# Splitting the negated row maxima on GpSimd instead of VectorE in a two-layer gated cross-attention kernel

## The reference, cut to what matters

```python
scores = jnp.einsum('bhqd,bhkd->bhqk', q, k) / jnp.sqrt(jnp.float32(HD))
scores = jnp.where(mask, jnp.float32(-1000000000000000.0), scores)   # layer 0 alone
attn = jax.nn.softmax(scores, axis=-1)
ctx = jnp.einsum('bhqk,bhkd->bhqd', attn, v)
```

## Time and profile before

| what | value |
|---|---|
| median of 3 runs | 342.97 us (339.25 to 344.19) |
| the profiled execution | 341.92 us |
| its span, first to last instruction | 339.7 us |
| PE busy | 280.9 us (83%) |
| VectorE busy | 213.8 us (63%) |
| ScalarE busy | 170.8 us (50%) |
| GpSimd busy | 92.1 us (27%) |

### The profile page before, as it was taken

How to read it: one execution, slowest core, us unless ns; L and a number is a source line. 1 busy time by engine, 2 the same in 40 slices (tenths; PEclk the granted TensorE clock), 3 DMA queues, 4 the chain that set the end, 5 groups by cost and what they waited for, 6 DMA issues and landing times.

```text
span 339.7 us, 7944 instructions
## 1 busy us (share of the span) xinstructions
PE 280.9 (83%) x2982; PEld 208.4 (61%) x2982; DVE 213.8 (63%) x658; ACT 170.8 (50%) x331; POOL 92.1 (27%) x158
## 2 busy tenths in 40 slices
PE   1723879899999999986999987899978887889870
PEld 0311556687778778764486465776766776768650
DVE  2310785676685676574447564774976885987890
ACT  1311226566655665645654542254767674676530
POOL 3510141152142241311000110431423431641450
PEclk9965878999999999999899999855999998999995
DMA  8366447444443332000000034344434443000121
GB/s 227 96 185 166 111 131 209 134 128 125 117 117 121 88 114 69 6 2 0 2 0 0 3 91 140 88 123 139 115 113 130 137 122 98 4 5 3 33 61 32
DMA packets 27679, 30.48 MB, mean 90 GB/s; under 512 B 13715, under 2 KB 24820, under 8 KB 26484
## 3 DMA queue, kind: packets, MB, share of 16 engines
q1 hardware_dynamic: 20446, 27.12, 27.6%
q10 hardware_dynamic: 4188, 2.47, 2.9%
q0 software_dynamic: 3008, 0.39, 0.8%
HBM read 22.43 MB, written 7.14 MB: 87 GB/s over the span
## 4 chain that ended last, share of the span: by engine, by line
PE 59%; DMA 12%; DVE 10%; POOL 6%; issue 5%; ACT 4%; ACTq 1%; SPq 1%; DVEq 0%; POOLq 0%
PE bank L1219 8%; DMA QS<-nmT 7%; PE bank L1189 6%; PE bank L1167 6%; PE bank L1311 5%; PE bank L1185 4%; PE bank L1163 4%; DMA QS<-qparts 3%; PE bank L1263 3%; PE bank L1227 3%; PE bank L1132 3%; PE bank L1245 2%; PE bank L1122 2%; DVE nmx L509 2%; POOL QS L402 2%
## 5 line engine op out<-in xcount | busy, mean ns | idle before, releaser
L509 DVE TENSOR_REDUCE nmx<-bank 128x4 f32<-128x480 f32 x128 | 82.9, 652 | 60.5 <-PE bank L1167 59.9
L920 ACT ACTIVATE P<-bank 120x512 f32<-120x512 f32 x128 | 76.4, 598 | 36.9 <-PE bank L1189 35.5
L402 POOL DMA_DIRECT2D QS<-nmT x94 | 46.2, 496 | 157.1 <-ACT nmT L911 157.1
L1189 PE MATMUL bank<-QS,KS 75*120 75x128 bf16 x512 | 53.6, 230 | 3.8 <-DMA QS<-nmT 3.4
L1189 PEld LDWEIGHTS bank<-QS,KS 75*120 75x120 bf16 x512 | 47.2, 142 | 11.9 <-issue 5.0
L1167 PEld LDWEIGHTS bank<-KS,QS 72*128 72x128 bf16 x512 | 41.4, 105 | 19.5 <-issue 9.2
L1167 PE MATMUL bank<-KS,QS 72*128 72x120 bf16 x512 | 52.3, 230 | 0.7 <-DVE nmx L509 0.7
L1219 PE MATMUL bank<-P,VS 120*32 120x128 f32 x1024 | 36.3, 284 | 4.3 <-DVE cn L544 3.1
L1219 PEld LDWEIGHTS bank<-P,VS 120*32 120x32 f32 x1024 | 27.5, 113 | 7.5 <-ACT P L920 4.6
L1163 PE MATMUL bank<-MB,IDH 128*128 128x480 bf16 x64 | 24.9, 389 | 6.1 <-DMA QS<-qparts 5.0
L1185 PE MATMUL bank<-IDH,MB 128*120 128x512 bf16 x64 | 26.0, 405 | 2.5 <-DMA QS<-nmT 2.2
(11 more groups left out here) (130 smaller groups left out, 448.6 us busy)
## 6 DMA issues: line engine op xcount, KB each, us to landing
KS<-kparts SPq DMA_DIRECT2D x48, 180.0 KB
QS<-qparts SPq DMA_DIRECT2D x42, 192.0 KB
kparts<-kp SPq DMA_DIRECT2D x24, 120.0 KB, 3.0
qparts<-qp SPq DMA_DIRECT2D x21, 128.0 KB, 3.8
QS<-nmT POOLq DMA_DIRECT2D x94, 4.0 KB, 2.8
QS<-qparts ACTq DMA_DIRECT2D x6, 192.0 KB
X<-in_x SPq DMA_DIRECT2D x3, 256.0 KB, 15.7
out<-X SPq DMA_DIRECT2D x3, 256.0 KB, 2.3
```

The lines of the kernel that those rows point to most:

```text
L402: po.dma_start(QS[G % 2][STACK + p:STACK + p + 1, k // 2, :, (k % 2) * S:(k % 2 + 1) * S], nmT[Bi % 2][p * H:(p + 1) * H, :]).then_inc(m_l ...
L509: ins = nc.vector.tensor_reduce(nmx[Bi % 2][:, UH * r:UH * r + UH], QS_BANK[U % 3][:, 0:UH * SK].rearrange("p (h k) -> p h k", k=SK), AX.X ...
L920: nc.scalar.activation(P[Bi % 2][:, hh, :], src, ACT.Exp, scale=SCALE).then_inc(exp_done, 1)
L1189: last = mm(o[0:SK, j * S:(j + 1) * S], KS[G % 2][0:ROWS, k // 2, h, (k % 2) * SK:(k % 2 + 1) * SK], QS[G % 2][0:ROWS, k // 2, h, (k % 2) ...
```

## The change

GpSimd gets a function `max_parts`, with the four split instructions of the same shapes. Each waits for the one before it on a new semaphore `np_c`, and the last raises `nm_ok`. It stands in GpSimd's program at the head of step s+1, ahead of `ln_rstd_` and of `max_rows`; for the last sequence it stands ahead of `x_difference(1)`. VectorE loses the four, and `context` keeps the reciprocal and the product.

```diff
+            def max_parts(Bi):
+
+                i = Bi % 2
+                po.wait_ge(max_done, UNITS * (Bi + 1))
+                if Bi >= 2:
+                    po.wait_ge(nt_done, Bi - 1)
+                po.tensor_copy(nmp[i][:, 0, :], nmx[i][:, :]).then_inc(np_c, 1)
+                po.wait_ge(np_c, 3 * Bi + 1)
+                if Bi >= 1:
+                    po.wait_ge(nm_ok, Bi)
+                po.tensor_tensor(nmr[:, :], nmx[i][:, :], nmp[i][:, 0, :], ALU.subtract).then_inc(np_c, 1)
+                po.wait_ge(np_c, 3 * Bi + 2)
+                po.tensor_copy(nmp[i][:, 1, :], nmr[:, :]).then_inc(np_c, 1)
+                po.wait_ge(np_c, 3 * Bi + 3)
+                po.tensor_tensor(nmp[i][:, 2, :], nmr[:, :], nmp[i][:, 1, :], ALU.subtract).then_inc(nm_ok, 1)
...
                 for s in range(B + 6 if L == 0 else B):
+                    if 1 <= s < B + 1:
+                        max_parts(L * B + s - 1)
                     if norm_at(L, s):
                         ln_rstd_(ln_no(*norm_at(L, s)))
                     if 1 <= s < B + 1:
...
                 else:
+                    max_parts(NB - 1)
                     x_difference(1)
                     max_rows(NB - 1)
...
-            def parts_and_normalise(Bi, Bn):
...
+            def context(Bn):
+
+                v.wait_ge(cb_done, Bn + 1)
+                if Bn >= 1:
+                    v.wait_ge(cn_ok, Bn)
+                if Bn >= 2:
+                    v.wait_ge(ct_done, Bn - 1)
+                pv = bank[4][:, :].rearrange("p (h c) -> p h c", c=VW)
+                link(nc.vector.reciprocal(rec[:, :], pv[:, :, HD]))
+                nc.vector.tensor_tensor(cn[Bn % 2][:, :].rearrange("p (h d) -> p h d", d=HD), pv[:, :, 0:HD],
+                                        rec[:, :].unsqueeze(2).broadcast_to([S, H, HD]), ALU.mult).then_inc(cn_ok, 1)
...
                         if r == 3 and 4 <= s < B + 4:
-                            parts_and_normalise(None, L * B + s - 4)
+                            context(L * B + s - 4)
...
-                    if s < B:
-                        parts_and_normalise(L * B + s, None)
```

More of the change, by code:

```diff
@@ L173, in gated_blocks @@
         v_done = sem("v_done"); v_evac = sem("v_evac"); bo_done = sem("bo_done"); bo_ok = sem("bo_ok")
-        qm_done = sem("qm_done"); max_done = sem("max_done"); nm_ok = sem("nm_ok")
+        qm_done = sem("qm_done"); max_done = sem("max_done"); nm_ok = sem("nm_ok"); np_c = sem("np_c")
         nt_done = sem("nt_done"); nt_evac = sem("nt_evac"); m_ld = [sem("m_ld0"), sem("m_ld1")]; m_last = sem("m_last")
@@ L726, in norm @@
                 def norm(b):
-                    parts_and_normalise(None, B + b)
+                    context(B + b)
                 mix_k(0)
```

## The result

| | before | changed |
|---|---|---|
| median (6 runs each) | 343.58 us | 346.13 us |
| lowest to highest | 339.25 to 346.42 | 344.89 to 350.14 |
| the profiled execution | 341.92 us | 346.05 us |
| its span | 339.7 us | 343.9 us |

A forecast was written before the change was run, and what follows sets the result against it. PE was taken as the bound, VectorE's work mattering only where the chain passes through it. Terms summed to +3.7 us: 345.6 from the profiled execution, 346.7 from the median, middle 346.1 us; 8-in-10 range 340.5 to 351.5.

The forecast's parts named there:

- What leaves VectorE brings nothing: The four split instructions, 26 us with gaps over 32 sequences, are almost nowhere on the path.
- the gain is real: Rival: VectorE's block is on the chain and the late root is hidden, about 4 us faster, 338.5; chance 0.2.
- The block on GpSimd: The four split instructions with handovers take 1.2 us on GpSimd, between 0.8 and 4.3.
- the block is dear: Rival: a slow bf16 conversion makes GpSimd's block 2 to 3 us, total 351 to 358; chance 0.13.
- Ordinary steps free: In steps without a norm the transpose has slack for the later split, so the change costs nothing.
- Layer 1, step 10: The split delays the root behind the bias addition, and the delay reaches PE at the values: +1.15 us.
- Layer 1, step 14: The same GpSimd queue delays the root, and the values at 298.42 idle for `cn`: +1.2 us.
- Layer 1, step 6: The same late root, less a VectorE gap of 0.45 us: +0.75 us at the values of 250.69.
- Layer 1, steps 1 and 2: The block waits for a row maximum ahead of the root; the transpose and first sequence's rows come later: +0.5 us.
- Layer 0, steps 1 and 2: Bias addition up to 0.65 us earlier, root 0.55 later, PE waits for a maximum behind the normalisation: +0.6 us.
- The end: The last split, on GpSimd ahead of the second `x_difference`, is done earlier than on VectorE: -0.5 us.
- The clock: Rival: longer waits bring one more half-clock stretch of about 10 us, losing 5 us, about 351; chance 0.1.

The follow-up runs named there:

- e4: The kernel before plus four spare split-shaped instructions on GpSimd ahead of the eight norm roots, nothing taken off VectorE: 1.0172 times the kernel before.
- e2: The changed kernel with the split of the eight sequences ahead of a norm back on VectorE, the other 24 on GpSimd: 1.0004 times the kernel before.
- e1: The changed kernel with the reciprocal root put ahead of the split in GpSimd's program: 0.9972 times the kernel before.
- e11: The changed kernel with eight splits ahead of norms back on VectorE and each root issued a step earlier, ahead of the bias addition: 1.0068 times the kernel before.
- e5: The changed kernel with `x_difference(0)` moved from the end of step 14 into step 15, behind the split: 1.0055 times the kernel before.
- e9: The kernel before with four spare GpSimd instructions ahead of the root at step 14 of layer 1 only: 1.0053 times the kernel before.
- e7: The kernel before, split still on VectorE, with each root issued at the end of the step before, ahead of the bias addition: 0.9945 times the kernel before.
- e8: The changed kernel as it is, measured once more among the experiments: 1.0068 times the kernel before.

## Why the prediction was right

The sum was +3.7 us on the profiled execution, and 4.1 were measured. Its mechanism was right, and the experiments carry it: e4 has the delay and nothing else, e2 the change without the delay. Its terms were less exact than their sum, and that the sum came so close is in part luck. As a share of the time, +3.7 us is 1.1% (the 346.1 us are 1.2% over the profiled execution, not 1.1%): inside the interval of the second measurement (0.1 to 1.2%) and below that of the first (1.3 to 2.6%).

- **What leaves VectorE brings nothing**: right. Busy time 194.8 instead of the 188 forecast. The forecast took off 26 us with the gaps between the four, which aren't busy time; the instructions themselves were 24.4. The normalisation (+1.1 us) and the mixing at the end (`FF<-FF,BC,xsh`, +0.9) took some back, and the rest is overlap with the neighbours that is gone. The rival *the gain is real* had 0.2; e1 at 0.9972 [0.9918, 1.0026] shows that even with no delay there is at most 0.8% of it.
- **The block on GpSimd**: priced 1.2 us, measured 1.05 to 1.07 in all but two places. The conversion to bf16, for which there was no row, takes 0.198 us: the row nearest in kind and size was the one to take, and the upper bound from the power was far off. The rival *the block is dear* fell with it.
- **Ordinary steps free**: right, TensorE never waits for L409 in one.
- **Layer 1, step 10**: +1.15 forecast, +0.87 in this execution (5.97 against 5.10 from V6 to V7). Over all traces it is 5.97 to 6.26 where the root is late and 5.09 to 5.82 where it isn't (e11, at 5.87, aside), about +0.7 between the middle ones. The mechanism is right, the price somewhat high. The sign given for it, TensorE's wait for `cn` over 1.2 us, didn't come: it is 0.61 at V7, 0.26 before.
- **Layer 1, step 14**: +1.2 forecast, +2.36 measured. The late root is 1.16 of it, as forecast; it reached TensorE at the transposes of the normalised x (the wait of 2.63 us), though, and not at the values behind `cn`. The other 1.20 is the step that failed. I followed the delayed instruction forward to who waits for it, and never asked beside what it would now run. I had cited the Trainium skill (SBUF — State Buffer, "SBUF: two separate sides") for the lock on the port pair and ruled that it leaves the sum as it is, because behind the fourth maximum VectorE reads PSUM. That holds for the neighbours of the split, except at the last one, where VectorE's mixing reads SBUF (0.58 us for a cast, shown below). The rule bit 3 us later, between a normalisation pushed back about 1.1 us and a GpSimd instruction that stayed. This case's trace agrees with the rule in that the two engines exclude each other: the normalisation takes 1.80 beside a GpSimd instruction of 1.05 and 0.59 without it (e5). It doesn't show the rule's order, that whichever starts first keeps the ports: by the records the stretched instruction had started first, at 294.78 against 295.18.
- **Layer 1, step 6**: +0.75 forecast; V2 to V3 took 5.75 before and 5.90 after, both at full clock, so in this pair of traces most of it didn't arrive. But one pair can't measure it: e9, which up to step 14 is the kernel before, took 4.74. Over all traces it is 5.58 to 6.25 in the six with the late root there and 4.74 to 5.77 in the others, and TensorE's wait for `cn` at V3 grew from 0.55 to 1.82 us (1.27 to 1.87 in the six; 0.55 to 0.67 in six of the eight others, 1.21 and 1.35 in e7 and e11). So the delay does arrive at TensorE here:

```profile
249.21 1.03 PE L1212 MATMUL bank<-P,VS 120*32 120x128 f32 x29 [1.82 <-DVE cn L542]
```

- **Layer 1, steps 1 and 2**: +0.5 forecast, +0.8 in V0. In e8, the same kernel, V0 starts at 229.49, earlier than in the kernel before, so this term isn't measured.
- **Layer 0, steps 1 and 2**: +0.6 forecast, none measured: V0 of layer 0 starts at 57.16 against 57.58. The sizes were wrong both ways. The bias addition didn't come 0.65 us earlier than at 45.09 but 1.58, and TensorE waited 1.97 us for the split behind it, which I hadn't listed:

```profile
43.51 1.25 POOL L378 TENSOR_TENSOR X<-X,tgbo 128x512 f32<-128x512 f32 x1 [1.86 <-DVE tgbo L559]
...
45.82 0.24 PE L1196 MATMUL bank<-IDH,nmp 128*48 128x128 bf16 x1 [1.97 <-POOL nmp L409]
46.01 1.03 POOL L370 TENSOR_TENSOR rstd<-ve,powT 128x4 f32<-128x4 f32 x1
```

  The root came 0.57 us earlier than before, not 0.55 later.
- **The end**: -0.5 forecast, not seen; with `values` at half clock (L1212 at 306.40, 1.94 us) TensorE had its own work until the transpose of 308.26, and V13 to the end is as long as before.
- **The clock**: the rival (0.1) asked for one more stretch at the lower level. There is none: apart from the drain the changed kernel has two from 215 us on, as before has (218 to 239 and 286 to 290 there, 218 to 232 and 296 to 310 here). The second was longer in this execution, and shorter in e8.

So the sum missed in three places: the stretched normalisation (+1.2), which I hadn't listed, the end (-0.5), which didn't come, and layer 0 (+0.6), which didn't arrive; step 6 (+0.75) and step 10 (+1.15) are of the right kind and not measured to some tenths. Too little on one side and too much on the other nearly cancelled, and where the clock fell in the two executions moved single stretches by 2 to 3 us.

## What to carry to other kernels

Before work is moved to an idle engine, read what stands behind it in that engine's order, not how idle the engine is: 0.2 us instructions cost nothing in 24 places and all of the loss in 8, where something that everybody waits for was queued behind them. If such a move is made, put the short, awaited instruction first (here the root): the same edit in that order cost nothing. And follow a delay twice, once to who waits for it and once to what will now run beside it; before two traces are subtracted step by step, lay their granted clocks side by side.

## What the runs showed of the hardware that wasn't expected

- When VectorE and GpSimd meet, one instruction is stretched by about what the other's still has to run, and it goes both ways. VectorE's normalisation (128x128 fp32, one tensor input in SBUF) took 1.80 us for a pair instead of 0.60 beside a subtraction of 1.05; its casts of 0.17 us took 1.33 beside a bias addition of 1.26 (e11) and 1.00 beside one of 1.29 (e9). GpSimd's own cast of 0.20 took 0.58 beside a VectorE instruction with two SBUF inputs, in the changed kernel's last split:

```profile
305.77 0.74 DVE L680 SCALAR_TENSOR_TENSOR FF<-FF,BC,xsh 128x512 f32<-128x512 f32 x1
305.99 0.58 POOL L407 CAST nmp<-nmr 128x16 bf16<-128x16 f32 x1
...
306.82 1.04 POOL L393 TENSOR_TENSOR XT<-xsh 128x512 f32<-128x512 f32 x1
306.83 1.58 DVE L688 SCALAR_TENSOR_TENSOR FF<-FF,BC,xsh 128x512 f32<-128x512 f32 x1
```

  The stretched one ends just behind the other, or at most its own length behind it: 305.99 + 0.58 is 306.57, just behind the end of L680 at 306.51, and L688 ends 0.55 us behind L393. Which of the two is stretched isn't told by the start records: the cast at 305.99 started later than its neighbour, the normalisation of step 14 (294.78 against 295.18) and the cast of e11 (291.88 against 291.91) earlier.
- On 128x16 fp32, GpSimd takes only a fifth to a quarter longer than VectorE: 0.198 against a median of 0.165 us for the cast, 0.213 to 0.218 against 0.175 for a subtraction.
